# Half-height score products, loads in one piece, filler products and a new list of steps in a two-block transformer on one core

## The reference

```python
# block 0: 16 heads of 16 channels
ada = silu(cond) @ Wada.T + bada          # gamma1, gamma2, scale1, scale2, shift1, shift2
qkv = (ln(x) * (scale1 + 1) + shift1) @ Wqkv.T + qkv_bias
qn, kn = q / |q| * sm, k / |k|            # per head
p = softmax(qn @ kn.T + attn_bias)
x = x + (p @ v @ Wproj.T + bproj) * gamma1
x = x + (gelu((ln(x) * (scale2 + 1) + shift2) @ Wfc1.T + bfc1) @ Wfc2.T + bfc2) * gamma2
# block 1: 4 heads of 64 channels
q, k, v = (rms_norm(x) * (cond @ norm_w.T + 1)) @ qkv_w.T
q, k = rope(cosine_scale(q, k, scale))
x = softmax(where(mask, q @ k.T, -1e30)) @ v @ out_w.T + x
```

## Time and profile before

| | |
|---|---|
| median of 3 runs | 268.47 us (265.78 to 269.16) |
| profiled execution, span from the first to the last instruction | 266.0 us (its whole time is not given apart) |
| busy in the span | PE 232.5, PEld 186.4, DVE 202.7, ACT 154.9, POOL 117.4 us |
| mean granted TensorE clock | 0.987 |
| by engine in the chain that ended last | PE 51%, DVE 16%, ACT 11%, issue 8%, POOL 7%, DMA 3% |
| moved by DMA | 10.11 MB |

### The profile page before, as it was taken

One profiled execution on the slowest core, in us unless ns is written; L12 is line 12 of the kernel. 1 busy time (PEld: TensorE's weight loads), 2 busy tenths in 40 slices (PEclk: granted clock), 3 DMA queues, 4 the chain that ended last, 5 costly groups with the idle time before them and its releaser, 6 DMA issues.

```text
span 266.0 us, 4823 instructions
## 1 busy us (share of the span) xinstructions
PE 232.5 (87%) x1710; PEld 186.4 (70%) x1710; DVE 202.7 (76%) x421; ACT 154.9 (58%) x303; POOL 117.4 (44%) x184
## 2 busy tenths in 40 slices
PE   0679788978998899899949999999998899989992
PEld 0658545736775678667738999999995767778682
DVE  4378969598994797797584486778799999997742
ACT  2301593447798898857894976811914564646520
POOL 8767973146062200801969237128226595650000
PEclk9999999599999999999999999999999999999999
DMA  5990000000800000000041000000000000001012
GB/s 172 374 276 0 4 1 0 0 1 3 315 5 7 1 2 5 2 0 5 2 122 33 11 1 2 0 0 2 0 2 1 0 5 0 0 2 39 0 42 79
DMA packets 8248, 10.11 MB, mean 38 GB/s; under 512 B 1824, under 2 KB 7072, under 8 KB 8224
## 3 DMA queue, kind: packets, MB, share of 16 engines
q1 hardware_dynamic: 8224, 9.79, 11.1%
HBM read 8.61 MB, written 1.05 MB: 36 GB/s over the span
## 4 chain that ended last, share of the span: by engine, by line
PE 51%; DVE 16%; ACT 11%; issue 8%; POOL 7%; DMA 3%; SPq 2%; ACTq 0%; DVEq 0%; POOLq 0%
PE ring L785 8%; PE ring L786 7%; PE ring L787 7%; PE ring L791 6%; PE ring L838 5%; PE psx L863 5%; PE pv L883 4%; DMA xs<-in_x 3%; PE ring L1047 3%; DVE nm L1153 3%; ACT kstk L673 3%; ACT kstk L672 2%; PE pv L1062 2%; ACT ps L598 2%; POOL nt L450 1%
## 5 line engine op out<-in xcount | busy, mean ns | idle before, releaser
L1153 DVE TENSOR_REDUCE nm<-ring 128x2 f32<-128x512 f32 x64 | 40.2, 683 | 5.3 <-PE ring L838 5.2
L598 ACT ACTIVATE ps<-psx 128x1024 f32<-128x1024 f32 x32 | 31.3, 1026 | 7.5 <-PE psx L863 4.3
L838 PE MATMUL ring<-kstk,qstk 128*128 128x512 f32 x64 | 25.0, 449 | 4.1 <-ACT kstk L673 2.7
L785 PE MATMUL ring<-wqkv_hi,xm_hi 128*128 128x512 f32 (+1 forms) x64 | 24.3, 379 | 4.4 <-DVE xm_lo L1146 2.9
L786 PE MATMUL ring<-wqkv_lo,xm_hi 128*128 128x512 f32 (+1 forms) x64 | 23.3, 364 | 0.0
L787 PE MATMUL ring<-wqkv_hi,xm_lo 128*128 128x512 f32 (+1 forms) x64 | 22.9, 358 | 0.0
L838 PEld LDWEIGHTS ring<-kstk,qstk 128*128 128x128 f32 x64 | 11.3, 193 | 13.9 <-DVE nm L1153 5.3
L791 PE MATMUL ring<-ident,stack 128*128 128x128 f32 x128 | 17.7, 278 | 2.9 <-ACT kstk L673 1.4
L863 PE MATMUL psx<-qstk,kstk 128*128 128x256 f32 x128 | 19.7, 287 | 0.3 <-ACT ps L598 0.3
L863 PEld LDWEIGHTS psx<-qstk,kstk 128*128 128x128 f32 x128 | 17.8, 189 | 2.5 <-ACT ps L598 0.9
L883 PE MATMUL pv<-ps,vs 128*32 128x256 f32 x256 | 16.1, 383 | 3.6 <-issue 3.3
(11 more groups left out here) (195 smaller groups left out, 695.6 us busy)
## 6 DMA issues: line engine op xcount, KB each, us to landing
xs<-in_x SPq DMA_DIRECT2D x4, 256.0 KB, 8.2
stage_a<-in_wada SPq DMA_DIRECT2D x4, 256.0 KB, 6.9
stage_a<-in_wfc SPq DMA_DIRECT2D x1, 1024.0 KB, 5.0
stage_b<-in_wfc SPq DMA_DIRECT2D x1, 1024.0 KB, 8.7
out<-x SPq DMA_DIRECT2D x4, 256.0 KB, 2.1
row<-in_rows SPq DMA_DIRECT2D x1, 906.0 KB, 8.8
stage_b<-in_wqkv SPq DMA_DIRECT2D x1, 768.0 KB, 7.0
stage_a<-in_wqkv SPq DMA_DIRECT2D x1, 768.0 KB, 4.5
```

Source lines behind the costliest of these rows:

```text
L598: a.activation(ps[:, n % 4], psx[:, n % 2], ACT.Exp).then_inc(exp_done, 1)
L785: mm(dst, lhs[0], rhs[0], start=start, stop=False)
L838: last = mm(dst, qstk[:, b % 2, p, qc * P:(qc + 1) * P], kstk[:, b % 2, 2 * p:2 * p + 2, :], start=True, stop=not with_bias)
L1153: v.tensor_reduce(nm[:, qc, :, p], bank(key).rearrange("p (h n) -> p h n", h=2), AX.X, ALU.max, negate=True).then_inc(ring_dve, 1)
```

## The change

Two heads of a pair now share kstk as they share qstk, without zeros. A score product takes only a head's 64 rows; the two heads of a pair alternate, and each writes a bank of its own. The `zeros` steps, and the second ACT copy of each transposed k, are gone. A step `max0` now holds one pair's two banks, each with one head and both query tiles, and claims both before its first product. w1 has a tile of its own.

The host lays every input out as the partitions will hold it, so each load is one piece per partition; x of batch 1 is loaded before the row vectors, these are shorter, and their zeros for k are written by POOL. qkv's weights are split in two steps, by rows of the weight. `busy` steps issue two products each of the identity with itself, 512 columns of bfloat16, into a psx bank that nobody reads. The list is redrawn; its rows as numbers tell little, so the first line of either stands below and the order on three engines after the diff.

```diff
-const_sel silu const_v zeros:0 stats0:0 norm0:0 ada split_wqkv0 normed0:0 head_scales split0:0 stats0:1
+busy:0 silu busy:1 const_sel busy:2 busy:3 busy:4 busy:5 const_v stats0:0 split_wqkv0:0 norm0:0 ada
...
-        return [(("mx", b, q // PAIRS, q % PAIRS), "dve") for q in (2 * i, 2 * i + 1)]
+        return [(("mx", b, i, par), "dve") for par in range(2)]
...
-        kstk = sb("kstk", [P, 2, H0, L], F32R)
+        kstk = sb("kstk", [P, 2, PAIRS, L], F32R)
+        w1_sb = sb("w1_sb", [P, 2, 2048], F32R)
...
+            sp.dma_start(stage_a[:, 1024:2048], wada[:, 1024:2048]).then_inc(s_wada, 16)
+            sp.dma_start(stage_b[:, 0:FC * 3 * C], wqkv).then_inc(s_wq, 16)
             load_x(1)
...
+            sp.dma_start(row[:, 0:C], rows[:, 0:C].to_broadcast([P, C])).then_inc(s_row, 16)
+            sp.dma_start(row[:, R_V:R_END], rows[:, C:C + R_END - R_V].to_broadcast([P, R_END - R_V])).then_inc(s_row, 16)
...
-                if name == "zeros":
-
-                    g.memset(kstk[:, b, :, :].bitcast(F32), 0.0).then_inc(kzero_ready, 1)
...
-                        src = bank(key).rearrange("p (a n) -> p a n", a=4)
-                        dst = kstk[:, b % 2, :, i_ * P:i_ * P + P].rearrange("p (a c) n -> p a c n", c=2)[:, 4 * u:4 * u + 4]
-                        a.activation(dst[0:SLOT, :, 0, :], src[0:SLOT], ACT.Copy)
-                        a.activation(dst[SLOT:P, :, 1, :], src[SLOT:P], ACT.Copy).then_inc(ring_act, 1)
+                        a.activation(kstk[:, b % 2, 4 * u:4 * u + 4, i_ * P:i_ * P + P],
+                                     bank(key).rearrange("p (a n) -> p a n", a=4), ACT.Copy).then_inc(ring_act, 1)
...
-                    act.wait_ge(s_full, 3 * PAIRS)
                     split_hi(s_w1, 16, w1_hi, stage_a[:, 0:FC * HID].rearrange("p (f n) -> p f n", f=FC))
...
+            def head_rows(par):
+
+                return slice(SLOT * par, SLOT * par + SLOT)
+
+            def max_scores(b, p, with_bias):
+
+                if p == 0:
                     for w in ("qT", "kT"):
                         pe.wait_ge(*emptied((w, TB * b + 1, 1)))
-                last = mm(dst, qstk[:, b % 2, p, qc * P:(qc + 1) * P], kstk[:, b % 2, 2 * p:2 * p + 2, :],
-                          start=True, stop=not with_bias)
...
+                dst = [claim(("mx", b, p, par)) for par in range(2)]
+                for qc in range(TB):
+                    for par in range(2):
+                        rows_ = head_rows(par)
+                        last = mm(dst[par][:, qc * L:(qc + 1) * L], qstk[rows_, b % 2, p, qc * P:(qc + 1) * P],
+                                  kstk[rows_, b % 2, p, :], start=True, stop=not with_bias)
...
-                for i in range(2):
-                    for kc in range(TB):
+                for kc in range(TB):
+                    for i in range(2):
                         keys = slice(kc * P, kc * P + P)
-                        last = mm(dst[:, i, kc, :], kstk[:, b % 2, 2 * p + i, keys], qstk[:, b % 2, p, :],
+                        last = mm(dst[:, i, kc, :], kstk[head_rows(i), b % 2, p, keys], qstk[head_rows(i), b % 2, p, :],
...
+            def keep_busy(count):
+
+                for _ in range(count):
+                    mm(psx[:, 0, 0], ident_b[:, :], ident_b[:, :].unsqueeze(1).to_broadcast([P, 4, P]),
+                       start=True, stop=True)
...
-                    split_lo(1, wqkv_hi, wqkv_lo, stage_b[:, 0:FC * 3 * C])
+                    split_lo(b + 1, wqkv_hi[:, b, :], wqkv_lo[:, b, :], stage_b[:, 3 * C * b:3 * C * (b + 1)])
```

255 lines of the change are left out of this document (125 added, 130 removed).

## The result

| | before | after |
|---|---|---|
| median of 19 runs each | 268.05 us (265.78 to 269.74) | 265.38 us (261.67 to 267.82) |
| ratio of after to before, 95% interval | | 0.984 (0.981 to 0.988) |
| profiled execution: span; mean granted clock | 266.0; 0.987 | 262.3; 0.967 |

By the ratio the change gains 1.6%, by the medians 1.0% (2.7 us): surely more than nothing, less than the 2% that I had called a difference, and far less than the forecast of 257 (250 to 265).

What follows compares the result with a forecast made beforehand. It took waits to bound the start, VectorE the next stage, ScalarE the scores and TensorE the rest; -5.2, -4.4, -2.1 and 0 summed to -11.7, a median of 257 us, range 250 to 265.

Steps and rivals of the forecast that it cites:

- From the last exponent on: Two-layer products and second block, to the end: same products on a full TensorE, 0, with 2 us either way.
- Start to first maximum: Kernel start: earlier weights and x, no memset, fewer PSUM copies and reordered VectorE work, -5.2 us.
- the case of 1.7 us: Start: if the clock is still low at the ten fillers, they last 4.3 us and the first product is 1.7 late.
- First maximum to first scores: Between these events: less VectorE work, fewer copies and no clock fall, 21.5 us against 25.9, so -4.4.
- No granted clock of 0.50 between: Sign: no granted clock of 0.50 between the first maximum and the first score product near 59 us.
- Scores: Score stage and tail: copies -4.7, earlier w1 subtraction -1.8, postponed bias adds +1.4, two-bank claim +3.0; sum -2.1 us.
- The forms: Score steps: halves overlap at 0.12 us a pair; changes between halves and full height cost 0.16 us each, 66 instead of 25.
- the halves are paid back by the ring: Rival: claim costs 6 us, kstk copies give only 2.3, start only 2.5; 265 us, chance 0.14.
- TensorE was the bound after all: Rival: in the scores TensorE's savings count instead of the copies, -8.4 for -4.7, later stages gain 2; 251, chance 0.07.
- The clock falls in the scores: Rival: idler TensorE brings spells at 0.50, up to 3.3 us each, three costing 10; 267 us, chance 0.05.
- Every change of form lies on the path: Rival: in the scores the 41 added changes cost their 6.6 us in full; 263.4 us, chance 0.05.
- The slower rival: Halves do not overlap and run at 0.21 us each, 64 steps costing 24 us more; near 287 us, chance 0.04.

Runs made afterwards that it cites:

- no_branch: one_bank without the branch on the bias flag and the second copy of the scores with bias: 259.70 us, ratio 0.966.
- one_bank: The changed kernel, but a step of maxima claims its second bank only after the products into the first: 260.77 us, ratio 0.970.
- scores_twice: one_bank with the four products of each score step issued twice: 266.03 us, ratio 0.992.
- no_fillers: The changed kernel without all 40 filler products: 266.23 us, ratio 0.992.
- copy_twice: one_bank with each kstk copy on ScalarE split into two of 64 rows, as the kernel before had them: 276.52 us, ratio 1.032.

## Why the prediction was wrong, step by step

The sum was -11.7, the profile shows -3.7; what lies around the span is 1.75 us (264.05 for 262.3) and not the 2.5 that I took. **The step that failed most is "From the last exponent on: 0."** It measured +4.2: 1.0 to the first fc1 product (6.30 for 5.32, by the spell behind the branch), 1.1 to the second block's scores (60.0 in ten of the eleven traces whose list is new there, 58.9 in all six under the old list), 2.3 to the last projection (62.5 for 60.2), of which the new order is 0.9 and most of the rest the spell at 211, and -0.1 behind it. So some 2.0 us belong to the order, and some 2.3 to two spells, which differ from execution to execution. I had taken this stage as "the same products on a full TensorE"; its time depends on how the engine comes into it, and no_branch shows that 2.3 us brought to its start can be lost inside.

*Start to first maximum, -5.2; measured -3.3.* The weights landed 1.4 earlier instead of 2.2. The wait for x is gone. From landing to first product it took 6.7 us instead of 5.26: the first half's low parts stand ahead of the normalisation (I had noted that and counted no change), and the ten fillers last 4.0 us at the low clock, 1.3 of these 1.4 us. That was the case of 1.7 us that I had named and not taken. The bias add gained 2.7 instead of 3.6, the rest 0.6 instead of 1.6, which I did not take apart.

*First maximum to first scores, -4.4; measured -1.7.* I had placed the claim's price in the scores alone. Here it is 0.4 (23.5 in two-bank traces without a spell, 23.1 in one_bank), and the spell at 42 takes 1.5. With neither, in one_bank, the stage gains 3.5. "No granted clock of 0.50 between" failed too.

*Scores, -2.1; measured -2.9.* Near in sum, wrong in parts. The claim cost 1.0 here (66.27 for 65.26); with the 0.4 before it 1.4, where I took 3.0, and 4.6 over the whole kernel's medians, spells and clock included, inside my bounds of 0 and 6. The halved copies were undersized: I took 2.4 and 4.7, and putting them back costs 15.7, some 12 of it at nearly equal clock. And "zero, because TensorE is waited for less" was wrong: TensorE time that scores_twice adds counts for two thirds of its size (4.9 of 7.2); what the halves saved was not measured by itself. These sizes do not add up to -2.9, and I did not take the rest apart.

*The forms.* The overlap was right (0.11 a pair; I took 0.12), and the change of form was 0.2 where I took 0.16, so that a step of maxima behind another form takes 0.43 and not 0.24 to 0.3. The Trainium skill, TensorEngine Tiling (Array Packing), section Tiling Modes under Key Properties, says that changing the mode drains the engine; the trace agrees, with that 0.2 us. My count of the changes was too high: between first and last score product the trace has 47, that of before 22, where I had 66 and 25, so 25 were added and not 41.

*The rivals.* The time is that of the first, "the halves are paid back by the ring", 265, and its mechanism ran (7.7 us of waits). But the number came out by luck: another of its parts was a small gain of the copies, which was large, and it had nothing behind the last exponent, where 4.2 were lost. "TensorE was the bound after all" is half true, by scores_twice. "The clock falls in the scores" missed the place: from 63.7 to 130 it was 1.00 in this trace, and fell ahead of and behind them; in those of no_branch and no_fillers it fell in the scores too. "Every change of form lies on the path" stays open, for no run takes the changes away: 25 of 0.2 us are 5, and if two thirds of TensorE's time count, as in scores_twice, an estimate is some 3 us. The slower rival did not come: halves overlap.

*What would show it.* Right: products 0.23 apart, and fewer kstk copies (four a batch; my "eight" counted those of q). Wrong: first qkv product at 15.02 and not 12 to 13, first maximum 38.77 and not 36 to 38, first score product 62.9 and not near 59, last exponent at 130.0 and not 126, and the stage behind it. VectorE's idle time before maxima is 3.2 us, near the 3 that I named, but that says nothing for the claim: it waits less for TensorE than before, 1.9 us for 5.2, and it is TensorE that waits. VectorE on the pages of before and after:

```profile
L1153 DVE TENSOR_REDUCE nm<-ring 128x2 f32<-128x512 f32 x64 | 40.2, 683 | 5.3 <-PE ring L838 5.2
L1154 DVE TENSOR_REDUCE nm<-ring 128x2 f32<-128x512 f32 x64 | 41.2, 687 | 3.2 <-PE ring L832 1.9
```

**Not settled.** What decides whether the clock falls at a given wait: the wait of 2.3 us in the second block was followed by a spell in the changed kernel and in no_branch, not in one_bank, and the stop at the branch in 14 traces of 17. Whether the two-bank claim brings spells of its own. And why the late fillers help one list and not the other.

## What to carry to other kernels

Where a step that made its results one buffer at a time now needs two of three buffers before it starts, look for the claim's wait in every stage where it occurs, and try the one-at-a-time claim first: here the ratios are 1.6% and 3.0%. The wait is not its price: by the medians the claim cost 3.1, 4.6 and 6.0 us where it brought waits of 5.7, 7.7 and 13.6. A gain ahead of a stage counts only if that stage hands it on, so look for what it waits for at its own end. Copies that free a shared ring can cost more than their own time (here some 12 us at nearly equal clock, for 9.5), since everything that is to be written into the ring waits behind them. And where the clock moves between runs, compare stretches that have no spell, or runs at one clock, before a difference is put down to the edit.

## What the runs showed of the hardware

- A copy of 64 partitions takes as long as one of 128: 592 ns for 64x512 (copy_twice), 608 for the changed kernel's 16 copies of 128x512.
- Idle TensorE can be paid for after the wait as well: 2.7 us at the branch, then 32 value products in 3.10 instead of 1.93 us at a granted clock of 0.50. It need not be: before, 3.3 us of idleness in the same place were followed by 1.93.
- Ten bf16 products of 512 columns issued as fillers into a spell at the lower clock took 4.01 us, 0.40 each, and held up the product behind them by 1.3 us.
